# Building a table of one-hot counts with the sources split in 64 and 98 instead of 128 and 49, each step as two matmuls of half the width

## What is computed

```
# layer norm of x + three graph convolutions
h = x @ W
m = h[src] * norm_src[:, None]
agg = segment_sum(m, dst, num_segments=n)
out = agg * norm_dst[:, None] + b            # twice with relu, once without
x = layernorm(x + ...)

# layer norm of x + one product layer
bf  = ssp(ssp(basis(dist) @ V1 + c1) @ V2 + c2)
msg = x[src] * edge_feat * bf * cut[:, None]
agg = segment_prod(msg, dst, num_segments=n)
x = layernorm(x + ssp(agg @ V3 + c3))
```

## Time and profile before

| | us |
|---|---|
| median of 3 runs | 4655.83 (4644.31 to 4661.99) |
| profiled execution | 4661.2 |
| its span | 4659.4 |
| VectorE, TensorE, ScalarE, GpSimd busy in the span | 3161.9, 3628.6, 2724.9, 1914.3 |
| the table's stage, TensorE's first to last step | 55.9 to 835.3 |
| busy in 44.8 to 836.0: VectorE, TensorE, ScalarE | 783.84, 683.49, 480.02 |

### The profile page before, as it was taken

The page is one execution under the profiler, slowest core; times in us unless marked ns, Lnnn a source line. Parts: engine busy times, 40 slices in busy tenths (PEclk is TensorE's granted clock), DMA queues, the critical chain, the costliest instruction groups (busy, mean ns, idle before and its releaser), DMA issues. The chain is left out here.

```text
span 4659.4 us, 67064 instructions
## 1 busy us (share of the span) xinstructions
PE 3628.6 (78%) x23091; PEld 2344.5 (50%) x23091; DVE 3161.9 (68%) x5677; ACT 2724.9 (58%) x4265; POOL 1914.3 (41%) x1883
## 2 busy tenths in 40 slices
PE   5888889899999999999998566666666666666663
PEld 4777777444554455444544344444444444444442
DVE  9999999423333233332312788888888888888886
ACT  3666665322222222222200899999999989999983
POOL 6222000401000000100011677777777777777774
PEclk9888888999999999999999778788777778878775
DMA  4333333778887888887875666666666666666762
GB/s 139 131 134 131 124 129 129 239 242 250 247 248 225 245 246 245 249 247 243 248 229 167 193 198 194 199 195 202 197 195 200 199 195 199 195 198 194 201 186 76
DMA packets 641678, 920.75 MB, mean 198 GB/s; under 512 B 69714, under 2 KB 423239, under 8 KB 641431
## 3 DMA queue, kind: packets, MB, share of 16 engines
q1 hardware_dynamic: 550727, 782.85, 52.2%
q0 software_dynamic: 59936, 119.71, 10.9%
q10 hardware_dynamic: 30768, 15.26, 1.2%
HBM read 674.96 MB, written 242.59 MB: 197 GB/s over the span
## 5 line engine op out<-in xcount | busy, mean ns | idle before, releaser
L1311 POOL DMA_INDIRECT hgat<-x_rows,edge_src x1564 | 1504.6, 962 | 490.1 <-issue 475.1
L953 PE MATMUL bank<-gran,hp 128*128 128x490 bf16 x7056 | 1504.1, 372 | 28.6 <-DVE hp L1098 28.6
L953 PEld LDWEIGHTS bank<-gran,hp 128*128 128x128 bf16 x7056 | 677.3, 96 | 822.7 <-DVE hp L1098 30.1
L815 POOL DMA_INDIRECT x_sb<-h_rows,last_i x147 | 138.7, 943 | 1503.6 <-DMA h_rows<-h_out 1469.1
L1388 PE MATMUL bank<-c_b,one_b 96*128 96x512 bf16 x309 | 140.2, 454 | 744.4 <-DVE efl L1454 677.1
L1439 DVE TENSOR_SCALAR bank<-rows_e,edge_same,edge_first 128x128 f32<-128x128 f32 x1564 | 645.1, 412 | 42.5
L611 PEld LDWEIGHTS bank<-hi_hot,lo_hot 128*128 128x128 bf16 x7840 | 546.0, 155 | 217.8 <-issue 69.6
L611 PE MATMUL bank<-hi_hot,lo_hot 128*128 128x49 bf16 x7840 | 574.1, 219 | 94.7 <-DVE hi_hot L403 93.4
L527 ACT CAST stage<-bank 128x490 bf16<-128x490 f32 x784 | 451.9, 577 | 308.1 <-PE bank L611 297.4
L1019 DVE TENSOR_SCALAR t<-bank,c_sb 128x512 f32<-128x512 f32 x82 | 61.6, 751 | 826.3 <-PE bank L928 816.6
L1388 PEld LDWEIGHTS bank<-c_b,one_b 96*128 96x128 bf16 x309 | 30.5, 99 | 1019.9 <-issue 984.1
(11 more groups left out here) (237 smaller groups left out, 4485.9 us busy)
## 6 DMA issues: line engine op xcount, KB each, us to landing
gran<-step_counts SPq DMA_DIRECT2D x336, 857.5 KB, 4.9
dist<-weight_by_step SPq DMA_DIRECT2D x391, 256.0 KB, 4.6
running_products<-rows_e SPq DMA_DIRECT2D x391, 256.0 KB, 3.7
step_counts<-stage SPq DMA_DIRECT2D x112, 857.5 KB
ef<-in_edge_attr SPq DMA_DIRECT2D x391, 224.0 KB, 4.2
hgat<-x_rows,edge_src POOLq DMA_INDIRECT x1564
kn<-keep_and_norm_of_steps SPq DMA_DIRECT2D x48, 490.0 KB, 6.8
edge_filter_times_attr<-g_out SPq DMA_DIRECT2D x82, 256.0 KB, 3.5
```

The lines of the kernel that those rows point to most:

```text
L953: last = nc.tensor.matmul(y, hp[:, 7 * g + i, part, :], gran[:, g, :, i * IS:(i + 1) * IS], start=first, stop=last_)
L1311: pool.indirect_dma_start(out=hgat[:, b % U, c, :], out_offset=None, in_=x1_d, in_offset=bass.IndirectOffsetOnAxis(ap=edge_src[:, b, c:c + ...
```

## The change

`lo` becomes the low 6 bits (64 values) and the rest 7 bits (98 values in use), so `lo_hot` is [128, 7, 64, 10] and `hi_hot` [128, 70, 98]. A source with rest h has its old 49-fold column h // 2 and goes to the upper or lower 64 partitions by h % 2; `rep_hi` is laid out so that the first 49 columns of `hi_hot` stand for even h and the last 49 for odd. Each step is now two matmuls with the same 64 weight columns: the even half into partitions 0 to 63 of the bank, the odd half into 64 to 127. The bank ends up with the same numbers at the same places, so what reads it is unchanged. The smaller `lo_hot` has no room for four lent arrays any more: `number_k` and `e_ang` move to `hi_hot`, `iota_k` to `stage`.

```
-            lo_hot = sbt("lo_hot", [P, 2, 7, P, GS], BF16)
-            hi_hot = sbt("hi_hot", [P, 2, IS, NT + 1], BF16)
-            rep_lo = sbt("rep_lo", [P, P, GS], BF16)
-            rep_hi = sbt("rep_hi", [P, NT + 1], BF16)
+            lo_hot = sbt("lo_hot", [P, 2, 7, LO, GS], BF16)
+            hi_hot = sbt("hi_hot", [P, 2, IS, 2 * NT], BF16)
+            rep_lo = sbt("rep_lo", [P, LO, GS], BF16)
+            rep_hi = sbt("rep_hi", [P, 2 * NT], BF16)
...
-            e_in, number_k, e_ang = (lent(lo_all, FIRSTS, n, F32) for n in range(3))
-            iota_k = lent(lo_all, FIRSTS, 3, I32)
+            e_in = lent(lo_all, FIRSTS, 0, F32)
...
+            number_k, e_ang = (lent(hi_all, OTHERS, n, F32) for n in range(2))
+            iota_k = lent(stage[:, 0].rearrange("p h s -> p (h s)"), 0, 0, I32)
...
-                    nc.vector.tensor_scalar(rep_hi[:], iota_f[:, 0:NT + 1], 1.0, None, ALU.add)
+                    for half in range(2):
+                        nc.vector.tensor_scalar(rep_hi[:, half * NT:(half + 1) * NT], iota_f[:, 0:NT], 2.0, 1.0 + half, ALU.mult, ALU.add)
...
-                        nc.vector.tensor_tensor(lo_hot[:, r], lo_of.unsqueeze(2).to_broadcast([P, 7, P, GS]),
-                                                rep_lo[:].unsqueeze(1).to_broadcast([P, 7, P, GS]), ALU.is_equal)
+                        nc.vector.tensor_tensor(lo_hot[:, r], lo_of.unsqueeze(2).to_broadcast([P, 7, LO, GS]),
+                                                rep_lo[:].unsqueeze(1).to_broadcast([P, 7, LO, GS]), ALU.is_equal)
+                        nc.vector.tensor_tensor(hi_hot[:, r].rearrange("p s (m e) -> p s m e", e=2),
+                                                hi_t[:, at, :].unsqueeze(2).to_broadcast([P, IS, NT, 2]),
...
-                        nc.vector.tensor_scalar(lo_i[:, 0:n, :], row, P - 1, None, ALU.bitwise_and
+                        nc.vector.tensor_scalar(lo_i[:, 0:n, :], row, LO - 1, None, ALU.bitwise_and
                                                 ).then_inc(s_lo, 1)
-                        link(nc.vector.tensor_scalar(hi_i[:, 0:n, :], row, 7, 63, ALU.arith_shift_right,
+                        link(nc.vector.tensor_scalar(hi_i[:, 0:n, :], row, 6, 127, ALU.arith_shift_right,
...
-                                            last = nc.tensor.matmul(banks[f % 4][:, s * NT:(s + 1) * NT],
-                                                                    lo_hot[:, u % 2, g, :, s],
-                                                                    hi_hot[:, u % 2, g * GS + s, 0:NT],
-                                                                    start=True, stop=True)
+                                            for half in range(2):
+                                                last = nc.tensor.matmul(
+                                                    banks[f % 4][half * LO:(half + 1) * LO, s * NT:(s + 1) * NT],
+                                                    lo_hot[:, u % 2, g, :, s], hi_hot[:, u % 2, g * GS + s, half * NT:(half + 1) * NT],
+                                                    start=True, stop=True)
```

More of the change, by code:

```diff
@@ L27 @@
 IS = 7 * GS
+LO = 64
 IH = NT * IS
@@ L182, in gnn @@
             lent = lambda tile, start, n, dt: tile[:, start + 2 * EPP * n:start + 2 * EPP * (n + 1)].bitcast(dt)
-            assert FIRSTS % 2 == 0 and FIRSTS + 8 * EPP <= 14 * P * GS
-            e_in, number_k, e_ang = (lent(lo_all, FIRSTS, n, F32) for n in range(3))
-            iota_k = lent(lo_all, FIRSTS, 3, I32)
+            assert FIRSTS % 2 == 0 and FIRSTS + 2 * EPP <= 14 * LO * GS
+            e_in = lent(lo_all, FIRSTS, 0, F32)
             e_dst, e_pk = (lent(hi_all, 0, n, I32) for n in range(2))
+            OTHERS = 4 * EPP + 2 * P + 2 * ST
+            assert OTHERS + 4 * EPP <= 2 * IS * 2 * NT and 2 * EPP <= NT * IS
+            number_k, e_ang = (lent(hi_all, OTHERS, n, F32) for n in range(2))
+            iota_k = lent(stage[:, 0].rearrange("p h s -> p (h s)"), 0, 0, I32)
             assert RB[1] * P + 2 * EPP + 2 * KT * P <= SP_
@@ L391, in _ @@
                     nc.vector.memset(stage[:, 1], 0.0).then_inc(s_zero, 1)
-                    nc.vector.tensor_copy(rep_lo[:], iota_f[:].unsqueeze(2).to_broadcast([P, P, GS]))
-                    nc.vector.tensor_scalar(rep_hi[:], iota_f[:, 0:NT + 1], 1.0, None, ALU.add)
+                    nc.vector.tensor_copy(rep_lo[:], iota_f[:, 0:LO].unsqueeze(2).to_broadcast([P, LO, GS]))
+                    for half in range(2):
+                        nc.vector.tensor_scalar(rep_hi[:, half * NT:(half + 1) * NT], iota_f[:, 0:NT], 2.0, 1.0 + half, ALU.mult, ALU.add)
                     nc.vector.tensor_scalar(strict[:], iota_f[0:ST, 0:ST], pcol[0:ST, 0:1], None, ALU.is_gt)
@@ L399, in hots @@
                         lo_of = lo_t[:, at].rearrange("p (g s) -> p g s", g=7)
-                        nc.vector.tensor_tensor(lo_hot[:, r], lo_of.unsqueeze(2).to_broadcast([P, 7, P, GS]),
-                                                rep_lo[:].unsqueeze(1).to_broadcast([P, 7, P, GS]), ALU.is_equal)
[L402 to L406, removed]
+                        nc.vector.tensor_tensor(lo_hot[:, r], lo_of.unsqueeze(2).to_broadcast([P, 7, LO, GS]),
+                                                rep_lo[:].unsqueeze(1).to_broadcast([P, 7, LO, GS]), ALU.is_equal)
+                        nc.vector.tensor_tensor(hi_hot[:, r].rearrange("p s (m e) -> p s m e", e=2),
+                                                hi_t[:, at, :].unsqueeze(2).to_broadcast([P, IS, NT, 2]),
+                                                rep_hi[:].rearrange("p (m e) -> p m e", e=2).unsqueeze(1).to_broadcast(
+                                                    [P, IS, NT, 2]), ALU.is_equal).then_inc(s_hots, 1)
                     dve.sem_inc(s_fill, 14)
```

## The result

The changed kernel takes 5298.11 us (median; 5296.29 to 5303.99) against 4655.24 us beside it: 1.1384 times, 95% interval 1.1371 to 1.1396, 643 us more. The forecast was 4741 us with a range of 4585 to 5160. The direction and the bound were right; the loss was put at 85 us, less than a seventh of what it is, and the time lies outside the range.

What follows compares the result with a forecast made beforehand. VectorE was taken as the bound, TensorE close behind. After the change TensorE binds: 112 turns of 7.49 us (839) plus 26 at table fills make 865 against 780, +85 us: 4741 us, range 4585 to 5160.

Steps and rivals of the forecast that it cites:

- VectorE's part: Building lo_hot and hi_hot: 2.48 and 3.72 us, 6.05 us a turn instead of 6.63, 65 us gained if VectorE still bound.
- The new bound: Table stage: TensorE's turn of 7.49 us exceeds VectorE's 6.05, so TensorE becomes the bound and VectorE waits.
- The switches: TensorE changing between the full-width count matmul and the 64-column halves: 0.12 us each way, 0.24 us a group.
- (a): Price of a half step on TensorE, a 64-column load with 49 streamed columns: 28 ns, so a pair takes 56.
- the far end of (a): Full-width loads go in as four parts of 32 columns side by side; a half takes 112 ns, about 6060 us; 7%.
- the 5% case: The two halves of a step run at once on TensorE, 28 ns a pair; VectorE binds again, 4591 us; 5%.
- today's share of 0.24 at the lower level: TensorE's lower clock (1.2 GHz) was taken for about 0.24 of the stage's time, giving a group of 1.07 us.
- each further tenth adds 13 us: Each further tenth of the stage at TensorE's lower clock adds 0.017 us a group, 13 us.
- the 865 us forecast for the stage: The table stage: 839 us of TensorE turns plus 26 us at six table fills, against 780 before.
- The second rival: On TensorE, a half load costs 53 ns, like 62 columns of f32, with switches of width as taken: 5133 us; 24%.

Runs made afterwards that it cites:

- hots_only: Changed kernel with each step one full-width matmul again, weight columns 10 bytes apart (other counts): 4996.90 us against 5064.91 for the kernel before, ratio 0.9867.
- more_counts: Changed kernel with two more 128 x 490 matmuls of zero weights ahead of each count matmul: 6356.81 us, on the chip where the kernel before takes 5065.
- one_half: Changed kernel with only the even half of each step computed: 5703.08 us, on the chip where the kernel before takes 5065 us.
- side_by_side: Changed kernel with a group's ten even halves first, then its ten odd halves: 6268.70 us, on the chip where the kernel before takes 5065 us.
- contiguous: Changed kernel with each half's 64 weight columns taken contiguously (other counts): 5213.70 us, on the chip where the kernel before takes 5065 us.
- switch_only2: Kernel before the change, plus one 64-column load and a one-column matmul of zeros ahead of each count matmul: 4836.24 us against 4655.95.
- count_halves: Changed kernel with the count matmul also split into two of 64 columns: 5409.39 us against 5064.91 for the kernel before, ratio 1.0658.
- pairs_and_counts: Changed kernel with lo_hot laid out for contiguous weight columns and the count matmul in halves: 4604.48 us against 4655.95 for the kernel before, ratio 0.9895.

## Why the prediction was wrong

**VectorE's part held**: 2.49 and 3.72 us, and 66 us off the stage when it is alone (hots_only; 65 forecast). **The new bound held**: TensorE. **The switches held in size**: 0.22 us a group in the kernel with nothing else, 0.24 forecast. In the changed kernel too: ten pairs at 0.113 and a count matmul that streams for 0.39 to 0.41 at the lower clock (the spacing in more_counts) are 1.52 to 1.54 of 1.78 us, which leaves 0.24 to 0.26. ScalarE stayed hidden: it waits for TensorE 947 us.

**The step that failed is (a), the price of a half.** I took the 56 ns of the full step, divided by two, as the time of 64 elements read. It isn't proportional to columns: a load of 64 columns 20 bytes apart takes 113 ns, twice the full-width load of 128 (one_half). This was the far end of (a), whose picture was four parts of 32 columns side by side: 32 columns then take 56 ns, and 64 in one line 113, 1.76 ns a column both times. The numbers fit that picture, and so do the traces' records of the loads: each load of line 611 before, and of the full-width steps of hots_only, is recorded as 4 runs of 32 columns, each of line 616 as one run of 64. That the four runs go in at the same time is inferred from the pace. I gave this case 7%. And the 5% case, that two halves overlap, is true as well: one_half and side_by_side show that neighbours in different halves load at once and neighbours in the same half do not. The two together, which no rival combined, make a pair of 113 ns instead of 56: 10 × 57 ns × 784 groups = 447 us.

What made the load dear is the distance of the columns, not the width alone: 113 ns at 20 bytes and 53 ns side by side, for the same 64 columns at the lower clock (contiguous). At full width the step took 56 ns at 20 bytes and 40 at 10 (hots_only). The working had noted that the 56 ns didn't follow the clock and drew nothing from it; in these runs the loads at 10 and 20 bytes don't follow the clock, and the contiguous ones do.

**The second term mis-sized is the clock.** I carried over today's share of 0.24 at the lower level. The changed kernel is there all the time. By the working's own group times, 1.07 us in today's shares and 1.20 at the lower clock, that is 0.13 × 784 = 102 us. I had named the direction ("each further tenth adds 13 us", which gives 99 for the rest of the stage) but only as an aside, and had written of a TensorE that might never be lowered. switch_only2 shows that two switches of width a group, with a matmul of one column, are enough to bring the lower clock to most of the stage; count_halves and pairs_and_counts show it rise when the switches go.

447 + 102 = 549 us, against the 560 between the 865 us forecast for the stage and the 1425 measured.

The second rival, 53 ns a half with switches (5133 us), came nearer to the 5298 than my own term, but by luck: it let twenty halves follow one another, and they go in pairs. Ten pairs at 53 ns would have given about my own forecast. What it was short of is the distance of the columns, which makes the pair 113 ns.

**Open:** what decides the clock. Three full-width count matmuls a group didn't raise it (more_counts), while before it was up most of the time with one. That switches of width bring the lower level here is shown; why they do is not. Idle time in general isn't it: TensorE was idle for 28% of the stage in pairs_and_counts, mostly at the full clock, and for under 1% in the changed kernel, always at the lower one. Also open is whether full-width weights with contiguous columns would do as well as the pairs: no run has them.

## What to carry to other kernels

The time of a weight load depends on how far apart its columns lie and on whether the load is of full width, and it isn't proportional to the number of columns: before narrowing it, look in the trace whether the steps' pace follows the clock, and lay the weight columns side by side. Halving the matmuls paid here (1%) only once they came in pairs for different halves of the array, with contiguous columns, and with nothing of another width between them. When TensorE gets new switches of width in a stage where it is close to the bound, work out the whole stage once at the lower clock, as a case and not as a remark.

## What the runs showed of the hardware that I had not expected

- A load of 64 bf16 columns: 113 ns with the columns 20 bytes apart, at both clocks; 53 ns with them side by side, at the lower clock. At the full clock a pair of contiguous ones took 32 ns. A full-width step: 56 to 58 ns at 20 bytes, 40 to 41 ns at 10 bytes, at both clocks.
- Two halves of the array load and multiply at the same time for the price of one (1420 us of stage with one half, 1425 with both); two matmuls of 64 × 490 end within 0.42 us.
- A pair of width switches, with a matmul of one column between them: 0.22 us a group, and the lower clock for 86% of the count matmuls of the stage (switch_only2).
- The granted clock doesn't follow TensorE's busy share: 99% busy at the lower clock in the changed kernel, 72% busy and mostly at the full one in pairs_and_counts.
- A profile can print a granted clock of 1.00 where the matmuls have the length of the lower one: 589 ns here, against 394 ns at the full clock; the stretch had no clock record.
